# v projected in the attention's prologue instead of in the query stage (Mamba block, attention and experts on one core)

## The chip, the cores and the metric

The kernel runs on one core of a Trainium2 chip, in one launch. The metric is the device time of that core in microseconds (us), the median of several runs. A second number is used beside it: the span of one profiled execution, from its first to its last instruction. The engines are named as in the profile: PE is the matrix engine, PEld its weight loads, DVE the vector engine, ACT the scalar engine, POOL the GpSimd engine, and SP issues most of the DMA transfers.

## What is computed

The input x is 2 sequences of 2048 tokens, 256 wide. First x gets a Mamba block added (a selective scan over 512 channels and 16 states). Then follows the part that the change touches, and after it a layer of 8 experts, two of which each token uses:

```python
f = layernorm(x)                        # over the 256 features
a = rmsnorm(f) * ln1_w
q, k, v = a @ wq.T, a @ wk.T, a @ wv.T  # 16 heads of 16 columns
probs = softmax(q k^T / sqrt(16))       # per sequence and head, 2048 x 2048
h = f + (probs @ v) @ wo.T
out = x + h + moe(rmsnorm(h) * ln2_w)
```

## The kernel before, in words

The program has four stages, one after the other: `ssm_stage` (the Mamba block), `qkv_stage` (normalisation and the projections to q, k and v), `attention_stage` and `moe_stage`. Between `qkv_stage` and `attention_stage` all engines meet: the first stage's block ends when the last of its engines is done.

**`qkv_stage`.** It goes over 8 chunks of 512 tokens, c = 2i + b, where b is the sequence and i the chunk in it. The step of a chunk (`every_chunk`, `step`) has these parts, and each engine does its own in the order of its program:

- DVE makes the statistics and norms of the *next* chunk (`Normed.norms`, L1072 to L1096). It ends with `an`. On the way it waits twice for a square root from ACT (L1047, L1053).
- PE turns `an` (8 transposes, L1268) into `tr_ps`. ACT scales that with ln1_w into `aT` (L1219), which has two slots, one for each b. PE multiplies `aT` by wq and wk (L1279) into `qk_ps`.
- q and k leave as three bf16 parts whose sum is the float32 value. ACT casts the first part (L1227, once for q and once for k), DVE subtracts it (`rest`, L1306, twice), ACT casts the second part (L1253), and POOL makes the third (L1202, one instruction over 128 x 2048). SP stores each part to `parts` in memory (L1162).
- Last, PE multiplies `aT` by wv (L1287, 8 matmuls in the program, 16 in the records) into `v_ps`, and ACT copies that with 4 copies into `v_all` (L1236), where the attention takes it from.

At the end of the stage SP issues 16 loads of the first head's operands (`Lead.sync`, L1344). It may do so as soon as all chunks of b = 0 are stored. Then it issues the last chunk's 6 stores.

**`attention_stage`.** For each of 16 pairs of heads (both sequences), a head needs the maximum of its scores before their exponentials. So the maxima of a head are made while the head before it is computed, and those of the first head in a prologue. The maxima run through `ring`, a PSUM buffer of two slots s = 0, 1: for each of 16 key tiles t and each s, PE fills a slot with two matmuls (L1629), which use one half of the array's rows each, and DVE reduces it (L1752). PE may fill a slot again once DVE has reduced it. When the 32 reductions are done, DVE combines them (L1759), PE turns the row (L1636), ACT copies it (L1595), POOL splits it (L1552, L1554) and SP sends it to `qs` (L1513). The rest of the prologue is 8 fills for the second head. Then head 0 starts: scores (L1650) into `s_ps` (3 banks), exponentials on ACT (L1610), and values (L1662) from `vst`, which POOL copies out of `v_all` (`columns`, L1546) at the beginning of its prologue.

Of the kernel before, what the change touches and what calls it, by code (L numbers as in the profile page):

```python
# [1097 lines left out]
        last.then_inc(self.s_a, 1)  # L1098


def qkv_stage(nc, normed, f_dram, parts_dram, v_all, lead):
    B, L, _ = f_dram.shape
    NI = L // CH
    NC = B * NI
# [2 lines left out]
    with ExitStack() as ctx:  # L1107
# [6 lines left out]
        def sem(name):  # L1114
            return ctx.enter_context(nc.semaphore(name))

        wq, wk, wv = normed.w
        ln1, an, fo = normed.ln1, normed.an, normed.fo
        ident = normed.ident
        normed.second(ctx)  # L1120
        aT = sb("aT", [P, 2, KM, CH])
        part = sb("part", [P, 2, 3, 2 * KM, CH], BF16)
        rest = sb("rest", [P, 2, 2 * KM, CH])
        tr_ps = ps("tr_ps", [P, KM, CH])
        qk_ps = ps("qk_ps", [P, 2 * KM, CH])
        v_ps = ps("v_ps", [P, TT, DM])

        s_w, s_a, s_f, s_fst, s_tr = normed.s_w, normed.s_a, normed.s_f, normed.s_fst, normed.s_tr
        s_set = sem("q_set")
        s_aT = sem("q_aT")  # L1130
        s_qk = sem("q_qk")
        s_v = sem("q_v")
        s_p1 = sem("q_p1")
        s_r = sem("q_r")
        s_p2 = sem("q_p2")
        s_p3 = sem("q_p3")
        s_pst = lead.s_pst
        s_vout = sem("q_vout")

        block = ctx.enter_context(nc.Block())  # L1140

# [68 lines left out]
        @block.scalar  # L1210
        def _(act):
            act.wait_ge(s_w, 64)

            def take_aT(i, b):
                c = 2 * i + b
                wait(act, s_tr, c + 1)
                wait(act, s_v, c - 1)
                for k in range(KM):
                    nc.scalar.activation(aT[:, b, k, :], tr_ps[:, k, :], ACT.Identity,  # L1219
                                         scale=ln1[:, k:k + 1]).then_inc(s_aT, 1)  # L1220

            def first_part(i, b, m):
                c = 2 * i + b
                wait(act, s_qk, 2 * c + m + 1)
                wait(act, s_pst[b], 16 * 6 * i)
                at = slice(m * KM, (m + 1) * KM)
                nc.scalar.copy(part[:, b, 0, at], qk_ps[:, at, :]).then_inc(s_p1, 1)  # L1227

            def take_v(i, b):
                c = 2 * i + b  # L1230
                wait(act, s_v, c + 1)
                for t in range(TT):
                    dst = v_all[:, b * HP:(b + 1) * HP, bass.ds(i * TT + t, 1), :]
                    dst = dst.rearrange("p a o (h w) -> p (a o) h w", h=2)[:, :, :, 0:HD]
                    src = v_ps[:, t, :].rearrange("p (a h w) -> p a h w", h=2, w=HD)
                    last = nc.scalar.copy(dst, src)  # L1236
                last.then_inc(s_vout, 1)

            def front(i, b):
                take_aT(i, b)  # L1240

            def step(i, b, i2, b2):
                c = 2 * i + b
                if b2 is not None:
                    normed.first_root(act, i2, b2)
                first_part(i, b, 0)
                if b2 is not None:
                    normed.second_root(act, i2, b2)
                first_part(i, b, 1)
                if b2 is not None:  # L1250
                    take_aT(i2, b2)
                wait(act, s_r, 2 * (c + 1))
                nc.scalar.copy(part[:, b, 1], rest[:, b]).then_inc(s_p2, 1)  # L1253
                take_v(i, b)

            every_chunk(front, step, act)

        @block.tensor
        def _(pe):
            pe.wait_ge(s_w, 64)  # L1260

            def front(i, b):
                c = 2 * i + b
                wait(pe, s_a, c + 1)
                wait(pe, s_aT, 2 * c)
                for k in range(KM):
                    for t in range(TT):
                        last = nc.tensor.transpose(tr_ps[:, k, t * P:(t + 1) * P],  # L1268
                                                   an[b][:, t, k * P:(k + 1) * P], ident[:, :])
                last.then_inc(s_tr, 1)  # L1270

            def step(i, b, i2, b2):
                c = 2 * i + b
                wait(pe, s_aT, 2 * c + 2)
                for m, w in enumerate((wq, wk)):
                    wait(pe, s_r, 2 * c + m - 1)
                    for o in range(KM):
                        for k in range(KM):
                            last = nc.tensor.matmul(qk_ps[:, m * KM + o, :], w[:, k, o * P:(o + 1) * P],  # L1279
                                                    aT[:, b, k, :], start=(k == 0), stop=(k == KM - 1))  # L1280
                    last.then_inc(s_qk, 1)
                if b2 is not None:
                    front(i2, b2)
                wait(pe, s_vout, c)
                for t in range(TT):
                    for k in range(KM):
                        last = nc.tensor.matmul(v_ps[:, t, :], aT[:, b, k, t * P:(t + 1) * P], wv[:, k, :],  # L1287
                                                start=(k == 0), stop=(k == KM - 1))
                last.then_inc(s_v, 1)

            every_chunk(front, step, pe)

# [70 lines left out]
        self.lead(sp, 0, 0)  # L1363


def attention_stage(nc, parts_dram, v_all, att, B, L, lead):
    NP = B * HP
    QC = L // CH
    KT = L // P
    KK = 2 * KT  # L1370
    LEAD = 4
    assert QC == 4 and KT % 2 == 0 and NP % 2 == 0 and NP >= 6
    ROWS = 6 * HD + 2
    SC = float(HD) ** -0.5
    SR = 3
# [2 lines left out]
    with ExitStack() as ctx:  # L1378
# [36 lines left out]
        s_hi = sem("a_hi")  # L1415
        s_nmr = sem("a_nmr")
        s_on = sem("a_on")
        s_rec = sem("a_rec")

        LOADS = 16 * 2 * 2 * 6  # L1420
# [112 lines left out]
        def _(pool):  # L1533
# [29 lines left out]
                                        ALU.mult).then_inc(s_on, 1)  # L1563

            def prologue():
                columns(0, 0)
                rows_of_max(0, 1, None)

            def head(n, it, par, hh, has_prev, has_next, has_then):
                if hh == 1 and has_next:  # L1570
# [10 lines left out]
        @block.scalar  # L1581
        def _(act):
            def read_acc(n, hh):
                wait(act, s_pv, KK * n + KT * (hh + 1))
                nc.scalar.copy(osb[:, hh, :], acc[:, :]).then_inc(s_o, 1)

            def take_output(head, tile, nth):
                wait(act, s_S, taken(head, tile))
                wait(act, s_on, nth)
                nc.scalar.copy(oraw[:, :], s_ps[:, tile % SR, :]).then_inc(s_exp, 1)  # L1590

            def take_row(head, tile, nth):
                wait(act, s_S, nth if tile < 0 else taken(head, tile))
                wait(act, s_nmr, nth - 1)
                nc.scalar.copy(rowf[:, :], s_ps[0:KT, tile % SR, 0:P]).then_inc(s_exp, 1)  # L1595

            def prologue():
                take_row(0, -1, 1)

            def head(n, it, par, hh, has_prev, has_next, has_then):  # L1600
                u = 2 * n + hh
                for t in range(KT):
                    k = hh * KT + t
                    if t == 1 and has_prev:
                        read_acc(n if hh == 1 else n - 1, 1 - hh)
                    wait(act, s_pv, KK * n + k - PR + 1)
                    for j in range(QC):
                        tile = tile_of(t, j)
                        wait(act, s_S, taken(u, tile))
                        nc.scalar.activation(prob[:, k % PR, j, :], s_ps[:, tile % SR, :], ACT.Exp,  # L1610
                                             scale=SC).then_inc(s_exp, 1)
                    if t == T_OUT and has_prev:
                        take_output(u, I_OUT, u - 1)
                    if t == T_ROW and has_next:
                        take_row(u, I_ROW, u + 2)

            every_head(act, prologue, head)
            read_acc(NP - 1, 1)
            wait(act, s_S, TILES * 2 * NP)
            wait(act, s_on, 2 * NP - 1)  # L1620
            nc.scalar.copy(oraw[:, :], s_ps[:, 0, :]).then_inc(s_exp, 1)

        @block.tensor
        def _(pe):
# [28 lines left out]
            def values(n, par, k):  # L1653
# [9 lines left out]
                                            prob[:, k % PR, j, :], start=(t == 0), stop=(t == KT - 1))  # L1663
                last.then_inc(s_pv, 1)

            def prologue():
                ct = Count(0, start=True)
                pe.wait_ge(s_op4[0], LOADS4)
                for t in range(KT):
                    for s in range(2):  # L1670
                        maxima(ct, 0, t, s)
                pe.wait_ge(s_id, 2)
                rows_of_max(0, -1, 1)
                pe.wait_ge(s_op4[1], LOADS4)
# [816 lines left out]
def build(nc, a, out):  # L2491
# [8 lines left out]
    with ExitStack() as ctx:  # L2500
        s_x1st = ctx.enter_context(nc.semaphore("s_x1st"))
        with ExitStack() as ctx2:
            normed = Normed(nc, ctx2, x1, a["ln1_w"], a["wqT"], a["wkT"], a["wvT"], s_x1st)
            ssm_stage(nc, a["x"], a["W_inT"], a["vectors"], a["W_xT"],
                      a["W_outT"], x1, b_rows, normed, s_x1st)
            att = ctx2.enter_context(nc.sbuf_tensor("att", [P, L // P, B * HP, 2 * HD], F32))
            with ExitStack() as ctx3:
                v_all = ctx3.enter_context(nc.sbuf_tensor("v_all", [P, B * HP, L // P, VW], F32))
                lead = Lead(nc, ctx3, parts, L)
                qkv_stage(nc, normed, f, parts, v_all, lead)  # L2510
                attention_stage(nc, parts, v_all, att, B, L, lead)
            moe_stage(nc, f, att, a["woT"], a["ln2_w"], a["gateT"], a["w1T"], a["w2T"], a["w3T"], xg, out,
                      (normed.an[0], normed.fo[0]), normed.ident)

# [28 lines left out]
```

## Time and profile before

| | |
|---|---|
| runs | 3106.29, 3106.02, 3105.07 us, median 3106.02 us |
| profiled execution | 3123.07 us, its span 3121.2 us |
| mean granted PE clock | 0.962 of full speed |
| `qkv_stage` | from 1025.7 to 1131.2 us of the span |
| prologue of the attention | from 1131.2 to about 1177 us |
| busy PE, DVE, ACT, POOL over the span | 91%, 79%, 63%, 33% |

The profiled execution is one run with the profiler on; its time is 17 us above the median, so stretches are compared with stretches of the same trace. A timeline row gives the start, the time from the first start to the last end of merged instructions, engine, line, operation, what it writes and reads, their number, and in brackets how long the engine had been idle and what ended that. A row of stretches gives the stretch and its length, the busy time and number of instructions of PE, PEld, DVE, ACT and POOL, the granted clock, the DMA share and GB/s. The granted clock is a share of 2.4 GHz: 1.00 is 2.4 GHz and 0.50 is 1.2 GHz.

### The profile page before, as it was taken

To read this page: it belongs to the slowest core of one execution; us is meant where nothing else is said; L and a number is where in the kernel's file an instruction comes from. 1 tells how busy PE (TensorE), PEld (TensorE's weight loads), DVE (VectorE), ACT (ScalarE), POOL (GpSimd) and SP (SyncE) were. 2 spreads that over 40 slices of the span, in tenths; PEclk is the share of its full clock that TensorE was granted. 3 is DMA by queue.
4 is the path that set the end of the run, shared out by engine and by line. 5 is a ranking of instruction groups with operands and counts; after the bars stand their busy time and mean duration, and the time that the engine had idled before them with its cause. 6 is when DMAs were issued, how large, how long until landed. Compare 5 with 4: busy or idle time off the path is not lost. (4 is left out here: it accounts for less than half of the span.)

```text
span 3121.2 us, 48073 instructions
## 1 busy us (share of the span) xinstructions
PE 2835.9 (91%) x14250; PEld 1220.9 (39%) x14251; DVE 2461.2 (79%) x2883; ACT 1963.7 (63%) x3570; POOL 1033.5 (33%) x507
## 2 busy tenths in 40 slices
PE   8899889899866969999999999999999987499998
PEld 3344334444322522222222222222222226499997
DVE  5999999999999668888888888888888824444443
ACT  4676665665643426888787877878788873244443
POOL 4978878879763220000000000000000003422222
PEclk9999999999999979999999999999999997699999
DMA  2111111111111542111111011111111004533332
GB/s 68 38 53 58 38 51 58 41 51 51 41 44 40 187 124 41 42 42 34 40 42 36 25 35 42 42 42 39 35 42 42 11 25 157 184 50 49 48 48 37
DMA packets 125209, 169.40 MB, mean 54 GB/s; under 512 B 25552, under 2 KB 87760, under 8 KB 125008
## 3 DMA queue, kind: packets, MB, share of 16 engines
q1 hardware_dynamic: 110992, 148.19, 16.3%
q0 software_dynamic: 13440, 18.16, 3.4%
q8 instruction: 104, 1.70, 0.2%
q14 instruction: 97, 0.79, 0.1%
q10 hardware_dynamic: 576, 0.55, 0.1%
HBM read 125.80 MB, written 40.74 MB: 53 GB/s over the span
## 5 line engine op out<-in xcount | busy, mean ns | idle before, releaser
L1752 DVE TENSOR_REDUCE nmh<-ring 128x2 f32<-128x1024 f32 x1024 | 1196.0, 1219 | 178.2 <-PE ring L1629 177.9
L1610 ACT ACTIVATE prob<-s_ps 128x512 f32<-128x512 f32 x2048 | 1073.0, 603 | 281.9 <-PE s_ps L1650 281.9
L413 POOL TENSOR_TENSOR bx<-u,bb 128x2048 f32<-128x2048 f32 x127 | 574.3, 4528 | 171.7 <-DVE h L889 171.7
L1650 PE MATMUL s_ps<-qs,ks 98*128 98x512 bf16 x2048 | 612.8, 387 | 17.2 <-issue 11.6
L889 DVE TENSOR_TENSOR_SCAN h<-dA,state,bx 128x512 f32<-128x512 f32 x512 | 616.5, 1264 | 11.9 <-ACT dA L674 7.8
L674 ACT ACTIVATE dA<-dt,aneg 128x512 f32<-128x512 f32 x512 | 351.5, 690 | 316.5 <-DVE h L889 311.7
L1662 PE MATMUL acc<-prob,vst 128*32 128x512 f32 x4096 | 548.8, 608 | 0.2 <-ACT prob L1610 0.2
L743 PE MATMUL y_ps<-h,ident 128*128 128x512 f32 x1024 | 476.0, 609 | 1.1 <-DVE h L896 1.1
L1650 PEld LDWEIGHTS s_ps<-qs,ks 98*128 98x128 bf16 x2048 | 149.2, 97 | 579.5 <-ACT prob L1610 478.3
L1629 PE MATMUL ring<-k,q 64*128 64x512 bf16 x2048 | 347.9, 395 | 27.8 <-DVE nmh L1752 19.6
L896 DVE TENSOR_TENSOR h<-h,c_ps 128x2048 f32<-128x2048 f32 x128 | 289.7, 2263 | 3.5 <-PE c_ps L722 3.2
L743 PEld LDWEIGHTS y_ps<-h,ident 128*128 128x128 f32 x1024 | 200.3, 196 | 223.5 <-issue 216.3
L1552 POOL CAST nmr<-a_rowf 16x128 bf16<-16x128 f32 x32 | 9.0, 280 | 747.9 <-ACT a_rowf L1595 747.9
L1629 PEld LDWEIGHTS ring<-k,q 64*128 64x128 bf16 x2048 | 81.4, 93 | 377.5 <-issue 204.3
L1562 POOL TENSOR_TENSOR att<-oraw,rec 128x256 f32 (+1 forms) x32 | 19.8, 619 | 622.4 <-DVE rec L1766 622.4
L2088 POOL DMA_INDIRECT out_x<-fo,token x72 | 112.4, 1562 | 299.4 <-DVE fo L2453 296.5
L2470 DVE TENSOR_TENSOR an<-sl,up_ps 128x512 f32<-128x512 f32 x72 | 49.6, 689 | 186.5 <-ACT sl L2177 186.5
L2271 PE MATMUL t_ps<-m_xT,work 128*128 128x128 f32 x1152 | 142.2, 277 | 0.4 <-ACT work L2164 0.4
L2271 PE MATMUL up_ps<-m_xT,work 128*128 128x128 f32 x1152 | 141.0, 276 | 0.0
L2271 PEld LDWEIGHTS t_ps<-m_xT,work 128*128 128x128 f32 x1152 | 136.0, 194 | 0.9 <-issue 0.8
L2281 PE MATMUL t_ps<-w,an 128*128 x576 | 136.1, 379 | 0.0
L2271 PEld LDWEIGHTS up_ps<-m_xT,work 128*128 128x128 f32 x1152 | 135.1, 193 | 0.0
(253 smaller groups left out, 2496.9 us busy)
## 6 DMA issues: line engine op xcount, KB each, us to landing
bb<-b_rows SPq DMA_DIRECT2D x128, 256.0 KB, 3.1
q<-parts SPq DMA_DIRECT2D x256, 64.0 KB, 2.1
parts<-part SPq DMA_DIRECT2D x48, 256.0 KB, 2.5
qs<-parts SPq DMA_DIRECT2D x192, 64.0 KB, 2.9
ks<-parts SPq DMA_DIRECT2D x192, 64.0 KB, 2.9
xt<-slots_in SPq DMA_DIRECT2D x72, 133.0 KB
k<-parts SPq DMA_DIRECT2D x256, 32.0 KB, 2.0
fo<-in_x SPq DMA_DIRECT2D x8, 512.0 KB, 4.3
```

Of the source, the lines that this page charges most:

```text
L413: nc.gpsimd.tensor_tensor(bx[:, n % BR], u[:, b], bb[:, n % RB, None, :].to_broadcast([P, KI, CH]), ALU.mult).then_inc(s_bx, 1)
L674: nc.scalar.activation(dA[:, d % 2, :], dt[:, b, d, :], ACT.Exp, scale=aneg[:, d, n:n + 1]).then_inc(s_da, 1)
L743: last = nc.tensor.matmul(y_ps[:, d, :], ident[:, :], h[:, n % HR, d, :], start=False, stop=(n == NS - 1))
L889: nc.vector.tensor_tensor_scan(h[:, n % HR, d, :], dA[:, d % 2, :], bx[:, n % BR, d, :], state[:, b, n, d:d + 1], ALU.mult, ALU.add).then_ ...
L896: nc.vector.tensor_tensor(h[:, n % HR], h[:, n % HR], c_ps[:, None, :].to_broadcast([P, KI, CH]), ALU.mult).then_inc(s_hc, 1)
L1610: nc.scalar.activation(prob[:, k % PR, j, :], s_ps[:, tile % SR, :], ACT.Exp, scale=SC).then_inc(s_exp, 1)
L1629: ins = nc.tensor.matmul(ring[:, s, half, :], q4[r, slot, t * P:(t + 1) * P], k4[r, slot, s * CH:(s + 1) * CH], start=True, stop=True)
L1650: nc.tensor.matmul(s_ps[:, tile % SR, :], ks[:, par, hh, t * P:(t + 1) * P], qs[:, par, hh, j * CH:(j + 1) * CH], start=True, stop=True).t ...
L1662: last = nc.tensor.matmul(acc[32 * j:32 * j + 32, :], vst[:, par, t, v0:v0 + 32], prob[:, k % PR, j, :], start=(t == 0), stop=(t == KT - 1))
L1752: nc.vector.tensor_reduce(nmh[:, slot, t, 2 * s:2 * s + 2], ring[:, s, :, :], AX.X, ALU.max, negate=True).then_inc(s_free[s], 1)
L2271: last = nc.tensor.matmul(dst[:, q % 2, m * P:(m + 1) * P], wu[:, q % 2, w, k, m * P:(m + 1) * P], xT[:, q % 2, k, :], start=(k == 0), sto ...
L2281: last = nc.tensor.matmul(o_ps[:, q % 2, 0:DM], midT[:, q % 2, m, :], w2[:, bass.ds(e, 1), m, :].rearrange("p o n -> p (o n)"), start=(m = ...
```

## The change

`qkv_stage` no longer makes v. Its `v_ps` and the semaphores of v go away. `aT` is no longer a tile of two slots, but holds all 8 chunks: it lies in the memory of `att`, the attention's output, which is written only later. So ACT and PE address it in the loop by i. The attention's prologue makes v: after the two fills of key tile t, PE multiplies 256 tokens of `aT` by wv (`values_of`, 4 matmuls in the program, 8 in the records) into one of the three banks of `s_ps`, 16 groups in all, and ACT copies each with two copies into `v_all` (`take_v`). Before PE turns the row of maxima it now waits for all groups' copies, and POOL copies `columns` after the row of maxima, not before it.

```diff
@@ qkv_stage, scalar
                 wait(act, s_tr, c + 1)
-                wait(act, s_v, c - 1)
                 for k in range(KM):
-                    nc.scalar.activation(aT[:, b, k, :], tr_ps[:, k, :], ACT.Identity,
-                                         scale=ln1[:, k:k + 1]).then_inc(s_aT, 1)
+                    dst = aT[:, bass.ds(i, 1), b, k, :].rearrange("p o n -> p (o n)")
+                    nc.scalar.activation(dst, tr_ps[:, k, :], ACT.Identity, scale=ln1[:, k:k + 1]).then_inc(s_aT, 1)
...
                 nc.scalar.copy(part[:, b, 1], rest[:, b]).then_inc(s_p2, 1)
-                take_v(i, b)
@@ qkv_stage, tensor
                 if b2 is not None:
                     front(i2, b2)
-                wait(pe, s_vout, c)
-                for t in range(TT):
-                    for k in range(KM):
-                        last = nc.tensor.matmul(v_ps[:, t, :], aT[:, b, k, t * P:(t + 1) * P], wv[:, k, :],
-                                                start=(k == 0), stop=(k == KM - 1))
-                last.then_inc(s_v, 1)
@@ attention_stage, gpsimd
             def prologue():
+                rows_of_max(0, 1, None)
+                pool.wait_ge(s_vout, GROUPS)
                 columns(0, 0)
-                rows_of_max(0, 1, None)
@@ attention_stage, scalar
+            def take_v(group):
+                b, t0 = group // (KT // 2), 2 * (group % (KT // 2))
+                wait(act, s_v, group + 1)
+                for t in range(2):
+                    dst = v_all[:, b * HP:(b + 1) * HP, t0 + t, :].rearrange("p a (h w) -> p a h w", h=2)
+                    src = s_ps[:, group % SR, t * DM:(t + 1) * DM].rearrange("p (a h w) -> p a h w", h=2, w=HD)
+                    last = nc.scalar.copy(dst[:, :, :, 0:HD], src)
+                last.then_inc(s_vout, 1)
             def prologue():
+                for group in range(GROUPS):
+                    take_v(group)
                 take_row(0, -1, 1)
@@ attention_stage, tensor
+            def values_of(group):
+                b, t0 = group // (KT // 2), 2 * (group % (KT // 2))
+                wait(pe, s_vout, group - SR + 1)
+                for t in range(2):
+                    i, at = (t0 + t) // TT, (t0 + t) % TT * P
+                    for k in range(KM):
+                        last = nc.tensor.matmul(s_ps[:, group % SR, t * DM:(t + 1) * DM], aT[:, i, b, k, at:at + P],
+                                                normed.w[2][:, k, :], start=(k == 0), stop=(k == KM - 1))
+                last.then_inc(s_v, 1)
             def prologue():
                 ct = Count(0, start=True)
                 pe.wait_ge(s_op4[0], LOADS4)
                 for t in range(KT):
                     for s in range(2):
                         maxima(ct, 0, t, s)
+                    values_of(t)
+                pe.wait_ge(s_vout, GROUPS)
                 pe.wait_ge(s_id, 2)
                 rows_of_max(0, -1, 1)
```

The order of PE's program in the attention's prologue, before (128x512 is the shape of what a matmul writes; `nm` is the row of maxima):

```order
L1629 MATMUL ring<-k,q 128x512 x64
L1636 MATMUL s_ps<-a_ident,nm 16x128
L1629 MATMUL ring<-k,q 128x512 x16
L1650 MATMUL s_ps<-qs,ks 128x512 x2
```

and with the change, where the first pair of rows stands 16 times in all:

```order
L1623 MATMUL ring<-k,q 128x512 x4
L1666 MATMUL s_ps<-wv,att 128x256 x4
L1623 MATMUL ring<-k,q 128x512 x4
L1666 MATMUL s_ps<-wv,att 128x256 x4
...
L1630 MATMUL s_ps<-a_ident,nm 16x128
L1623 MATMUL ring<-k,q 128x512 x16
L1644 MATMUL s_ps<-qs,ks 128x512 x2
```

Between every four fills of `ring` now stand four matmuls of v.

ACT's program in the loop of `qkv_stage`, the step of an even chunk, before (ISA and REGISTER_ALU are register work):

```order
L1219 ACTIVATE aT<-tr_ps,ln 128x512 x2
L30 ISA
L1253 CAST part<-rest 128x2048
L1236 ISA
L1236 COPY v_all<-v_ps 128x8x2x16
L1236 ISA
L1236 COPY v_all<-v_ps 128x8x2x16
...
L1047 ACTIVATE q_sd<-q_mv,q_epsc 128x4
```

and with the change:

```order
L1215 ISA
L1215 ACTIVATE att<-tr_ps,ln 128x512
L1215 ISA
L1215 ACTIVATE att<-tr_ps,ln 128x512
L30 ISA
L1238 CAST part<-rest 128x2048
L30 ISA
L1047 ACTIVATE q_sd<-q_mv,q_epsc 128x4
```

The four copies of v are gone from between the cast and the square root, and a register instruction stands before each of the two writes of `aT`.

## Rows read from the trace of the kernel before

**Rows 1.** Busy time by stretch, a chunk of the query stage and the prologue.

```profile
1053.30:1065.10 11.80, 11.41 (x42) 6.83 (x41) 8.90 (x22) 6.76 (x11) 4.00 (x1) 1.00 0.66 214
...
1131.20:1168.30 37.10, 19.27 (x64) 3.28 (x64) 36.30 (x33) 0.00 (x0) 9.83 (x6) 0.50 0.29 78
```

**Rows 2.** Timeline of one chunk of the query stage, all engines.

```profile
1053.61 1.20 ACT L1236 COPY v_all<-v_ps 128x256 f32 x4 [0.44 <-PE v_ps L1287]
...
1059.43 1.14 DVE L1096 TENSOR_SCALAR an<-fo,q_rr 128x256 f32<-128x256 f32 x4 [0.20 <-DVE q_rr L1091]
1060.48 2.35 DVE L1306 TENSOR_TENSOR rest<-qk_ps,part 128x1024 f32<-128x1024 f32 x2
...
1060.70 1.09 PE L1268 MATMUL tr_ps<-ident,an 128*128 128x128 f32 x8 [0.39 <-DVE an L1096]
...
1061.63 3.62 PE L1287 MATMUL v_ps<-wv,aT 128*128 128x256 f32 x16
1061.83 1.26 ACT L1219 ACTIVATE aT<-tr_ps,ln 128x512 f32<-128x512 f32 x2 [0.47 <-PE tr_ps L1268]
...
1062.99 1.90 ACT L1253 CAST part<-rest 128x2048 bf16<-128x2048 f32 x1
...
1065.09 3.60 PE L1279 MATMUL qk_ps<-aT,wq 128*128 128x512 f32 x8
```

**Rows 3.** POOL's timeline: second, third and seventh of its eight subtractions.

```profile
1053.24 4.07 POOL L1202 TENSOR_TENSOR part<-rest,part 128x2048 bf16<-128x2048 f32 x1 [7.75 <-ACT part L1253]
1065.17 4.07 POOL L1202 TENSOR_TENSOR part<-rest,part 128x2048 bf16<-128x2048 f32 x1 [7.87 <-ACT part L1253]
...
1112.77 4.07 POOL L1202 TENSOR_TENSOR part<-rest,part 128x2048 bf16<-128x2048 f32 x1 [7.86 <-ACT part L1253]
```

**Rows 4.** DVE around POOL's second subtraction, and the same product without POOL beside it.

```profile
1008.13 0.16 DVE L1082 TENSOR_TENSOR q_ms<-q_mv,q_rs 128x4 f32<-128x4 f32 x1
...
1055.24 2.09 DVE L1082 TENSOR_TENSOR q_ms<-q_mv,q_rs 128x4 f32<-128x4 f32 x1
```

**Rows 5.** Timeline at the end of the query stage: SP and PE.

```profile
1119.78 0.35 SPq L1344 DMA_DIRECT2D q<-parts  x1
...
1127.13 3.56 SPq L1162 DMA_DIRECT2D parts<-part  x6
1131.24 1.04 PE L1629 MATMUL ring<-k,q 64*128 64x512 bf16 x4 [8.06 <-PEq L1107]
```

**Rows 6.** Timeline of the attention's prologue: PE, DVE and ACT.

```profile
1131.89 36.29 DVE L1752 TENSOR_REDUCE nmh<-ring 128x2 f32<-128x1024 f32 x32 [9.86 <-PE ring L1629]
1133.17 0.61 PE L1629 MATMUL ring<-k,q 64*128 64x512 bf16 x2 [0.89 <-DVE nmh L1752]
...
1165.97 0.61 PE L1629 MATMUL ring<-k,q 64*128 64x512 bf16 x2 [0.52 <-DVE nmh L1752]
1168.66 0.37 PE L1636 MATMUL s_ps<-a_ident,nm 128*16 128x128 f32 x1 [2.08 <-DVE nm L1759]
```

**Rows 7.** PE's timeline at full clock, in head 0 (starts tell the spacing).

```profile
1199.06 0.39 PE L1629 MATMUL ring<-k,q 64*128 64x512 bf16 x2
1199.38 0.82 PE L1650 MATMUL s_ps<-qs,ks 98*128 98x512 bf16 x3
1200.14 0.39 PE L1629 MATMUL ring<-k,q 64*128 64x512 bf16 x2
```

**Rows 8.** PE's timeline at the start of the query stage.

```profile
1025.88 1.07 PE L1268 MATMUL tr_ps<-ident,an 128*128 128x128 f32 x8 [1.81 <-PEq L67]
...
1028.36 5.31 PE L1279 MATMUL qk_ps<-aT,wq 128*128 128x512 f32 x8 [1.42 <-ACT aT L1219]
```

**Rows 9.** PE's first scores of head 0, and stretches around two rises of the clock.

```profile
1177.10 1.04 PE L1650 MATMUL s_ps<-qs,ks 98*128 98x512 bf16 x2
...
1028.40:1032.40 4.00, 4.00 (x6) 1.83 (x7) 1.78 (x8) 0.21 (x1) 0.00 (x0) 0.60 1.03 357
...
1184.40:1188.40 4.00, 3.62 (x21) 0.69 (x17) 2.38 (x3) 2.65 (x5) 0.00 (x0) 0.90 0.95 119
```

More of the change, by code:

```diff
@@ L1098, in norms, with qkv_stage @@
         last.then_inc(self.s_a, 1)
-def qkv_stage(nc, normed, f_dram, parts_dram, v_all, lead):
+def qkv_stage(nc, normed, f_dram, parts_dram, v_all, lead, aT):
     B, L, _ = f_dram.shape
@@ L1115, in sem @@
             return ctx.enter_context(nc.semaphore(name))
-        wq, wk, wv = normed.w
+        wq, wk = normed.w[0:2]
         ln1, an, fo = normed.ln1, normed.an, normed.fo
@@ L1120, in qkv_stage @@
         normed.second(ctx)
-        aT = sb("aT", [P, 2, KM, CH])
         part = sb("part", [P, 2, 3, 2 * KM, CH], BF16)
@@ L1125, in qkv_stage @@
         qk_ps = ps("qk_ps", [P, 2 * KM, CH])
-        v_ps = ps("v_ps", [P, TT, DM])
         s_w, s_a, s_f, s_fst, s_tr = normed.s_w, normed.s_a, normed.s_f, normed.s_fst, normed.s_tr
@@ L1131, in qkv_stage @@
         s_qk = sem("q_qk")
-        s_v = sem("q_v")
         s_p1 = sem("q_p1")
@@ L1137, in qkv_stage @@
         s_pst = lead.s_pst
-        s_vout = sem("q_vout")
         block = ctx.enter_context(nc.Block())
@@ L1227, in first_part @@
                 nc.scalar.copy(part[:, b, 0, at], qk_ps[:, at, :]).then_inc(s_p1, 1)
-            def take_v(i, b):
-                c = 2 * i + b
-                wait(act, s_v, c + 1)
-                for t in range(TT):
[L1233 to L1237, printed above, removed]
             def front(i, b):
@@ L1279, in step @@
                             last = nc.tensor.matmul(qk_ps[:, m * KM + o, :], w[:, k, o * P:(o + 1) * P],
-                                                    aT[:, b, k, :], start=(k == 0), stop=(k == KM - 1))
+                                                    aT[:, bass.ds(i, 1), b, k, :].rearrange("p o n -> p (o n)"),
+                                                    start=(k == 0), stop=(k == KM - 1))
                     last.then_inc(s_qk, 1)
@@ L1283, in step @@
                     front(i2, b2)
-                wait(pe, s_vout, c)
-                for t in range(TT):
-                    for k in range(KM):
-                        last = nc.tensor.matmul(v_ps[:, t, :], aT[:, b, k, t * P:(t + 1) * P], wv[:, k, :],
-                                                start=(k == 0), stop=(k == KM - 1))
-                last.then_inc(s_v, 1)
             every_chunk(front, step, pe)
@@ L1363, in sync, with attention_stage @@
         self.lead(sp, 0, 0)
-def attention_stage(nc, parts_dram, v_all, att, B, L, lead):
+def attention_stage(nc, normed, parts_dram, v_all, att, aT, B, L, lead):
     NP = B * HP
@@ L1371, in attention_stage @@
     LEAD = 4
-    assert QC == 4 and KT % 2 == 0 and NP % 2 == 0 and NP >= 6
+    assert B * KT // 2 == KT and QC == 4 and KT % 2 == 0 and NP % 2 == 0 and NP >= 6
     ROWS = 6 * HD + 2
@@ L1417, in attention_stage @@
         s_on = sem("a_on")
+        s_v = sem("a_v")
+        s_vout = sem("a_vout")
+        GROUPS = B * KT // 2
         s_rec = sem("a_rec")
@@ L2506, in build @@
             att = ctx2.enter_context(nc.sbuf_tensor("att", [P, L // P, B * HP, 2 * HD], F32))
+            aT = att[:, :, :, :].rearrange("p t a w -> p (t a w)")
+            aT = aT.rearrange("p (i b k n) -> p i b k n", b=B, k=KM, n=CH)
             with ExitStack() as ctx3:
@@ L2509, in build @@
                 lead = Lead(nc, ctx3, parts, L)
-                qkv_stage(nc, normed, f, parts, v_all, lead)
-                attention_stage(nc, parts, v_all, att, B, L, lead)
+                qkv_stage(nc, normed, f, parts, v_all, lead, aT)
+                attention_stage(nc, normed, parts, v_all, att, aT, B, L, lead)
             moe_stage(nc, f, att, a["woT"], a["ln2_w"], a["gateT"], a["w1T"], a["w2T"], a["w3T"], xg, out,
```

## The prediction

> **What bounds the kernel now.** I read the stretches first, to see which engine is full where v leaves and where it arrives. In a chunk of the query stage PE is busy 11.41 of 11.80 us, so it looks as if PE set the pace there; in the attention's prologue DVE is busy 36.3 of 37.1 us and PE only half of it, at a granted clock of 0.50 [rows 1]. The change looks right on both counts: it takes work from a full PE and gives it to a half idle one.
>
> The timeline of a chunk says otherwise. PE does not start its transposes when it is free, but when DVE's `an` is there: it idles 0.39 us before them [rows 2]. What `an` waits for is POOL. The small product `q_ms` (128 x 4) takes 0.16 us alone, but 2.09 us when it starts at 1055.24, and it ends at 1057.33; POOL's subtraction runs from 1053.24 to 1057.31 [rows 3, 4]. DVE stands still until POOL is done, whenever its product starts. So the chunk's period is a chain through DVE, ACT and POOL: `rest` ends at 1062.83; 0.16 later ACT's cast starts, 1.90; 0.28 later POOL starts, 4.07 [rows 2, 3]; from POOL's end (1057.31) to the end of `an` (1060.57) 3.26; from there to the end of `rest` 2.26 [rows 2, 4]. Sum 11.93 us. POOL's starts are (1112.77 - 1065.17)/4 = 11.90 us apart [rows 3]. v is in none of these terms.
>
> The stage's end is not PE's either. SP starts the first head's 16 loads at 1119.78, which need the parts that POOL made from 1112.77 on [rows 3, 5], issues the last stores until 1130.69, and then the attention starts, at 1131.24, with PE idle for 8.06 us [rows 5].
>
> In the prologue the reductions follow each other every 36.29/32 = 1.13 us, 2.26 per key tile [rows 6].
>
> **What leaves the query stage.** Per chunk PE loses 16 records of v. They start 3.46 us before the next matmuls, so 0.216 each [rows 2]. ACT loses four copies, 1.20 us [rows 2]. PE then waits for `aT`, which ends at 1063.09, and starts its next matmuls about 1.8 us earlier than 1065.09 [rows 2]. The cover that made v free is the DVE-POOL chain, and it stays: ACT's square root comes about 1.5 us earlier, so `q_ms` is issued earlier, but still after POOL has started, since the same cast precedes both [rows 2, 4]. The gain is **0 us** per chunk. The ends: 0, and PE's own loop if the chain did not bind (a rival below). The last chunk's v ended long before SP did [rows 5]: 0.
>
> **What the query stage gets.** ACT has a register instruction before each of its two writes of `aT`, and PE before two matmuls. PE's are covered by its new idle time. ACT's are not: `an`, transposes, `aT`, cast is a chain that ties with the one over `rest` (`aT` ends at 1063.09, the cast starts at 1062.99, `rest` ended at 1062.83 [rows 2]). No row prices them there. From below it is 0, since the second can go under the first write; from above 0.20 per chunk, DVE's idle time before `an` [rows 2]. I take 0.07, nearer to the lower end because ACT waits for the transposes anyway: 7 x 0.07 = **+0.5 us**, ends 0 and 1.4. The SP queue issues the same transfers in the same order.
>
> The clock of this stage can fall. Between the end of one chunk's q and k matmuls and the start of the next there will be about 4.7 us with only 1.1 us of transposes. At the stage's start PE had such a stretch, and the clock was at half for most of the 4 us that follow; the 8 matmuls then took 5.31 us, not 3.60 [rows 2, 8, 9]. That costs 1.7 us per chunk, against 1.8 us by which they start earlier: covered, and counted as 0.
>
> **What the prologue gets.** PE is to do 32 fills and 16 groups of 8 records of v. The clock decides. At 1.2 GHz a pair of fills streams for 0.43 us (its halves run side by side, 0.61 with the tail [rows 6]); at 2.4 GHz pairs end in 0.39 and the next group starts 0.32 later, 0.10 more than the 0.216 of a 512 column stream, and going back costs the same 0.10 ((1200.14 - 1199.38) - 3 x 0.22) [rows 7]. With v PE is nearly always streaming, so I expect 2.4 GHz after the start: the clock rose 3 to 4 us after dense matmuls began at 1028.36 [rows 8, 9].
>
> At full clock one key tile goes like this. From the first fill to its reduction 0.43 us (0.39 and 0.04), the second reduction starts 1.13 later, and its slot is refilled 1.28 after that (1133.17 - 1131.89 [rows 6]): 2.84 us from the first fill of a tile to the second fill of the next one. From there PE needs 0.32 for the fill and the change of kind, 8 x 0.216 = 1.73 for v and 0.10 to change back, 2.15 us, to the first fill of the tile after. Two tiles take 4.99 us, a tile **2.49 us** instead of 2.26. Neither engine is full: each waits for the other because the ring has only two slots. 16 x 0.23 = +3.7 us.
>
> The start is slower: at half clock a tile costs PE 2 x 0.43 + 2 x 1.73 + 0.2 = 4.5 us, so in the first 5 us it gets 1.1 tiles done, not 2.0; 0.9 x 2.49 = +2.2 us, ends 1.2 and 3.4 for a rise after 3 us, as there, or after 8, as in head 0, where scores began at 1177.10 and the clock rose about 1185.2 [rows 9]. At the end, the row of maxima turned 2.69 us after the last fill started (1168.66 - 1165.97 [rows 6]); now it waits for v, 2.05 us, the tail and semaphore, 0.2, and two copies on ACT, 0.6, with 0.1 behind them: 2.95, which is +0.3. The half clock's first tile had its first v wait covered by the first reductions: -0.6. Sum **+5.6 us**. ACT's 32 copies (0.6 per tile) are covered by the tile's 2.49. POOL's `columns` now stands behind the row of maxima; it is needed only by the first values of head 0, behind 8 more reductions of 1.13: 0. After that the order is the same, and head 0 starts at half clock in both; if it starts at the full one, up to 3 us come back.
>
> **The sum:** 0 + 0.5 + 5.6 = +6.1 us. Against the profiled execution 3123.1 + 6.1 = 3129.2; against the median of the runs, 17 us lower, 3106.0 + 6.1 = 3112.1, I say **3112.0 us**. A measurement of this kernel tells a change of about 0.2%, 6.2 us, from none, so the forecast lies at that edge.
>
> **The rivals.**
>
> *PE was the bound of the query stage.* The busy share speaks for it [rows 1]; the 0.39 us before the transposes and the 2.09 us product speak against it [rows 2, 4]. Then a chunk takes PE's loop: transposes to `aT` 1.13, `aT` 1.26, 16 matmuls at 0.43 6.9, handovers 0.3, sum 9.6, and 7 x 2.3 = 16.1 us come back: 3106.0 + 5.6 - 16.1 = 3095.5 us. Chance 0.07.
>
> *The prologue stays cheaper.* Changing kinds of matmul costs nothing (-1.5), the clock rises after 3 us (-1), and head 0 starts at full clock (-2): about +1.5, 3107.5 us. Chance 0.26.
>
> *The prologue is dearer.* Weight loads of v's float32 operand show behind a fill, where only bf16 changes have a row [rows 7]: 0.2 more per tile, half of which the coupling takes, and the clock rises late: +10, 3116 us. It decides once a tile takes over 2.55 us. Chance 0.20.
>
> *The clock of the query stage falls before the transposes too.* The row says that it fell in the stretch that held 8 transposes and idle time [rows 8, 9]. Where it covers the transposes of each chunk they take about 1 us longer on the chain: 7 us more, 3119 us. Chance 0.06. The Trainium skill speaks against the change here: its page "TensorE: Matmul & The Clock Gate", Part 4, says that a transpose on PE doesn't count as busy for the clock gate, so the whole gap would be idle for it. By that rule this rival comes out; in the row above the fall came after transposes, which agrees but doesn't prove it.
>
> *The clock never rises in the prologue,* as it did not rise there before [rows 1]. A tile costs 4.5 us: 16 x 2.24 = +36, 3142 us. Against it: v fills the gaps that kept PE half idle. Chance 0.03.
>
> **How the numbers follow.** The forecast's case (+4.5 to +8) has 0.38. Faster by over 0.2% is the first rival alone, 0.07. Slower is the dearer prologue, the two clock rivals and somewhat under half of the forecast's own case: 0.20 + 0.06 + 0.03 + 0.16 = 0.45. The rest, 0.48, is within 0.2%. The range runs from 3104 (the cheap prologue with all it can give back) to 3120 (the fallen clock), and leaves out PE's rival and the clock that never rises.
>
> **What would show it.** Right: POOL's subtractions still 11.9 us apart, `q_ms` still about 2 us and longer than before, PE idle about 3 us per chunk; the attention starting 105 to 107 us after the query stage; the 32 reductions spread over 41 to 44 us instead of 36.3; a granted clock of 1.00 in most of the prologue. Wrong: POOL's starts closer than 11.5 us, or reductions that still follow every 1.13 us.

## The result: 0.28% slower, by the prologue

Over 13 runs of each, the changed kernel took 3114.57 us and the kernel before 3105.78. The ratio is 1.0028, with a 95% interval of 1.0021 to 1.0036, so about 8.8 us more (6.5 to 11.2). The forecast was 3112.0. The runs of one kernel spread over 7 to 10 us, so the places are read from stretches inside one profiled execution. Over kernels with the same code there, they repeat within 0.3 us from the first fill on, and within 0.9 us in the query stage (106.44, 106.36 and 105.61 us in the changed kernel and in experiments 1 and 2):

| stretch | before | changed |
|---|---|---|
| query stage: PE's first transposes to its first fill of `ring` | 105.36 | 106.44 |
| prologue: first fill to the turned row of maxima | 37.42 | 44.02 |
| turned row to the first scores of head 0 | 8.44 | 8.11 |
| first scores to the first values | 6.09 | 6.10 |
| sum, us | 157.31 | 164.67 |

7.4 us of the loss stand here, 6.6 of them in the prologue. Of the 1.1 in the query stage 0.7 is one set of transposes that ran slowly once (experiment 7). The other 1.4 us are within the interval, and no stretch shows them: from its first to its last exponentials the attention took 1384 to 1390 us in the ten profiled executions, in no order by kernel. The totals of the profiled executions are not compared, since what follows the attention, which the change does not touch, took 559 us in that of the kernel before and 540 in that of the changed one, and the experiments show both lengths (540 in 1 to 4, 557 to 561 in 5 to 8).

The query stage after the change. First POOL's subtractions, the first four and the seventh (start, duration, engine, line, what, idle before and what ended it), to be laid beside [rows 3]:

```profile
1043.55 4.06 POOL L1198 TENSOR_TENSOR part<-rest,part 128x2048 bf16<-128x2048 f32 x1 [14.74 <-ACT part L1238]
1056.11 4.06 POOL L1198 TENSOR_TENSOR part<-rest,part 128x2048 bf16<-128x2048 f32 x1 [8.49 <-ACT part L1238]
1068.13 4.07 POOL L1198 TENSOR_TENSOR part<-rest,part 128x2048 bf16<-128x2048 f32 x1 [7.96 <-ACT part L1238]
1080.02 4.06 POOL L1198 TENSOR_TENSOR part<-rest,part 128x2048 bf16<-128x2048 f32 x1 [7.82 <-ACT part L1238]
...
1115.92 4.07 POOL L1198 TENSOR_TENSOR part<-rest,part 128x2048 bf16<-128x2048 f32 x1 [7.96 <-ACT part L1238]
```

They are 12.56, 12.02 and 11.89 us apart, and (1115.92 - 1056.11)/5 = 11.96 on average from the second on. PE lost 3.46 us of work per chunk and the chunk did not get shorter. The small product that waits for POOL shows why. This is the answer for the tile `q_ms` in the changed kernel (number, shortest, median and longest in ns, first and last start):

```profile
L1082 DVE TENSOR_TENSOR q_ms<-q_mv,q_rs x6: 3716/3771/3936, 1043.9 to 1104.2; 128x4 f32<-128x4 f32 x6
```

Beside POOL's subtraction it starts about 1.6 us sooner than before, and it takes 1.6 us longer (3.7 against 2.09 in [rows 4]): it still ends when POOL ends.

The prologue after the change, its start, a steady piece and its end, PE and DVE:

```profile
1134.36 1.03 PE L1623 MATMUL ring<-k,q 64*128 64x512 bf16 x4 [13.32 <-PEq L1107]
...
1135.33 3.78 PE L1666 MATMUL s_ps<-wv,att 128*128 128x256 f32 x8
...
1139.04 1.04 PE L1623 MATMUL ring<-k,q 64*128 64x512 bf16 x4
...
1141.93 0.61 PE L1623 MATMUL ring<-k,q 64*128 64x512 bf16 x4
...
1142.36 4.82 DVE L1758 TENSOR_REDUCE nmh<-ring 128x2 f32<-128x1024 f32 x4 [0.32 <-PE ring L1623]
1142.47 1.99 PE L1666 MATMUL s_ps<-wv,att 128*128 128x256 f32 x8
...
1144.39 0.77 PE L1623 MATMUL ring<-k,q 64*128 64x512 bf16 x4
...
1145.09 1.99 PE L1666 MATMUL s_ps<-wv,att 128*128 128x256 f32 x8
...
1147.02 0.61 PE L1623 MATMUL ring<-k,q 64*128 64x512 bf16 x4
...
1147.45 4.82 DVE L1758 TENSOR_REDUCE nmh<-ring 128x2 f32<-128x1024 f32 x4 [0.28 <-PE ring L1623]
...
1174.94 0.78 PE L1623 MATMUL ring<-k,q 64*128 64x512 bf16 x4
...
1178.38 0.28 PE L1630 MATMUL s_ps<-a_ident,nm 128*16 128x128 f32 x1 [0.74 <-ACT v_all L1586]
```

and the stretches up to and from the rise of the clock (PE, PEld, DVE, ACT, POOL busy, granted clock, DMA share, GB/s):

```profile
1134.30:1140.10 5.80, 5.74 (x17) 2.91 (x17) 2.77 (x3) 0.65 (x2) 5.66 (x4) 0.51 0.66 175
1140.10:1178.40 38.30, 37.56 (x177) 24.18 (x177) 35.14 (x31) 9.71 (x30) 3.59 (x2) 1.00 0.21 50
```

The first two tiles, at 1.2 GHz for most of the time, take 1141.93 - 1134.36 = 7.57 us. Two tiles of the steady part took 4.52 before: +3.0. (The first two tiles before took less, 4.19 us, because both slots are free at the start. Against them it is +3.4, and the end gives 0.4 back.) The 13 tiles from there to the last take 1174.94 - 1141.93 = 33.0, so 2.54 each against 2.26: +3.6. In the steady piece DVE's reductions come in fours, with a gap of 0.27 us before the next four. PE waits less. It goes from fill to fill in 1144.39 - 1141.93 = 2.46 us in one tile and 1147.02 - 1144.39 = 2.63 us in the next, where the four fills take 0.77 us instead of 0.61 because a slot is not free yet. So PE's own work alone would take about 2.46 us per tile, 0.20 more than DVE's 2.26, and the waits for each other add only the last 0.08. The turned row waited for ACT's last copy, as the last row says, but by little: it came 1178.38 - 1174.94 = 3.44 us after the last tile's first fill, against 3.82 before, and DVE had finished the row of maxima only 0.3 us earlier, at 1178.07.

### The profile page after: what moved, and what is told of

Its sections match the earlier page's. It is cut to its first block and busy times, and to the rows that moved or that the text cites. A ratio compares the mean times of both kernels' runs of the same rounds, so it can differ in the third digit from the quotient of the medians.

```text
span 3115.0 us, 48067 instructions
## 1 busy us (share of the span) xinstructions
PE 2846.5 (91%) x14250; PEld 1223.7 (39%) x14251; DVE 2471.8 (79%) x2883; ACT 1964.3 (63%) x3570; POOL 1033.5 (33%) x507
## 5 line engine op out<-in xcount | busy, mean ns | idle before, releaser
L743 PE MATMUL y_ps<-h,ident 128*128 128x512 f32 x1024 | 483.9, 617 | 1.1 <-DVE h L896 1.1
L1623 PE MATMUL ring<-k,q 64*128 64x512 bf16 x2048 | 340.0, 388 | 17.4 <-PEq L1107 13.3
```

What stands on the lines that cost most here:

```text
L743: last = nc.tensor.matmul(y_ps[:, d, :], ident[:, :], h[:, n % HR, d, :], start=False, stop=(n == NS - 1))
L1623: ins = nc.tensor.matmul(ring[:, s, half, :], q4[r, slot, t * P:(t + 1) * P], k4[r, slot, s * CH:(s + 1) * CH], start=True, stop=True)
```

## The experiments

Experiments 1 to 4 were timed beside the kernel before at 3105.95 us, 5 to 8 beside it at 3126.93 us; a ratio is always to the runs of the kernel before that were made beside it. Times of stretches are those of the table above.

### 1. No v at all

```diff
-                    values_of(t)
-                pe.wait_ge(s_vout, GROUPS)
...
-                for group in range(GROUPS):
-                    take_v(group)
...
-                nc.gpsimd.memset(v_all[:, :, :, col:col + 1], 1.0).then_inc(s_set, 1)
+                nc.gpsimd.memset(v_all[:, hh * HP:(hh + 1) * HP, :, :], 1.0).then_inc(s_set, 1)
```

> The changed kernel without v: no matmuls and no copies of v anywhere, v_all is set to ones. It tells what the query stage alone gives. Theory 1 (the pace of the query stage is the chain DVE, ACT, POOL): POOL's subtractions 11.9 to 12.1 us apart as in the changed kernel, the prologue back at 37.4 us from the first fill to the turned row, so the kernel before + 1 us (+0 to +2), and 7 to 8 us faster than the changed kernel. Rival (PE was the bound of the query stage): 9.6 us per chunk, 15 us faster than before.

Measured: 1.0004 (0.9995 to 1.0013). The query stage took 106.36 us, the prologue 37.42, the whole stretch 158.30, which is 1.0 above the kernel before. A kernel that makes no v at all is not faster than one that makes it in the query stage. So v was free where it stood, and the rival (15 us faster) is out.

### 2. Half of v in the prologue

```diff
-                    for k in range(KM):
-                        last = nc.tensor.matmul(s_ps[:, group % SR, t * DM:(t + 1) * DM], aT[:, i, b, k, at:at + P],
-                                                normed.w[2][:, k, :], start=(k == 0), stop=(k == KM - 1))
+                    last = nc.tensor.matmul(s_ps[:, group % SR, t * DM:(t + 1) * DM], aT[:, i, b, 0, at:at + P],
+                                            normed.w[2][:, 0, :], start=True, stop=True)
```

> The changed kernel with half of v's matmuls: only the first 128 of the 256 features are summed; groups, copies, waits and changes of kind stay. Theory 1 (two slots of the ring couple PE and DVE: two tiles cost the 2.84 us of the reductions plus what PE does after the refill): 2.84 + 0.3 + 0.86 + 0.3 = 4.3 us is under DVE's own 4.52, so the reductions follow every 1.13 us once the clock is up, prologue 37.4 + 1 to 3 us, the kernel 4 to 5 us faster than the changed one. Rival (each group has a fixed cost by its waits, its weight loads or ACT's reads of PSUM beside DVE's): tiles stay at about 2.5 us, no gain over the changed kernel beyond 1 us.

Measured: 1.0002 (0.9993 to 1.0011), prologue 38.60 us, 5.4 less than with all of v. Once the clock is up, the reductions run as before, here ten in 11.40 us:

```profile
1138.51 0.61 PE L1623 MATMUL ring<-k,q 64*128 64x512 bf16 x4
1138.94 11.40 DVE L1757 TENSOR_REDUCE nmh<-ring 128x2 f32<-128x1024 f32 x10 [0.38 <-PE ring L1623]
```

The groups, their waits, their changes of kind and ACT's copies are all still there and cost nothing here. What costs is PE's time between two fills once it is longer than the reductions leave it. The 1.2 us that stay are about the start at half clock. This experiment does not tell the coupling by two slots from PE's own time: the shorter groups bring PE's own time to about 1.6 us per tile as well, also under DVE's 2.26. The rows of the result tell them apart (2.46 and 2.54 us), and a ring with a third slot was not tried.

### 3. and 4. POOL's subtraction behind DVE's norms

In the kernel before (3) and in the changed one (4):

```diff
             def third_part(i, b, norms_after=True):
...
+                if norms_after:
+                    wait_apart(pool, s_a, c + 3, s_w)
                 nc.gpsimd.tensor_tensor(part[:, b, 2], rest[:, b], part[:, b, 1], ALU.subtract).then_inc(s_p3, 1)
```

The last two subtractions have no norms to wait for. They stand behind the loop without the new wait.

> The kernel before with one more wait: POOL's subtraction of chunk c waits until DVE has made an of chunk c + 2 (so that DVE's norms are never beside POOL's read). All is computed. Theory 1 (POOL's subtraction holds DVE's norms up): q_ms takes 0.16 us again, the chain gets shorter than PE's work, and PE's 11.4 us per chunk bind: 0.3 to 0.5 us per chunk, 2 to 3.5 us faster than before. Rival (DVE's long q_ms is something else, POOL is not what it waits for): POOL's work is only later, the chunk gets longer by up to 4 us, 0 to 28 us slower than before.

> The changed kernel with the same wait of POOL. Theory 1: with the chain shortened, PE has room (no v) and the chunk falls to 9.7 to 10.5 us: 10 to 15 us faster than the changed kernel, 1 to 6 us faster than the kernel before. Together with the run before this one it tells that v's matmuls cost the query stage something only where the chain does not bind. Rival (PE's own loop or the clock binds near 11.9): under 3 us faster than the changed kernel.

Measured (3): 0.9997 (0.9988 to 1.0006), which alone says nothing. The stretches do: the query stage took 102.53 us, 2.8 less, and `q_ms` takes 0.16 us:

```profile
L1082 DVE TENSOR_TENSOR q_ms<-q_mv,q_rs x6: 161/162/164, 1044.1 to 1100.2; 128x4 f32<-128x4 f32 x6
```

Measured (4): 0.9993 (0.9984 to 1.0003), against 1.0028 for the change without the wait; the query stage took 98.74 us, 7.7 less than in the changed kernel. POOL made to wait makes the stage shorter, in both kernels, so POOL's work beside the norms was what held them. And v's matmuls show their price now: with the chain shortened, the stage takes 3.8 us longer with v (102.53) than without (98.74).

The gain is under the 10 us that I had expected, and the trace of (4) says where it went. Third to fifth of POOL's subtractions, and PE's and DVE's rows around them:

```profile
1067.78 4.08 POOL L1200 TENSOR_TENSOR part<-rest,part 128x2048 bf16<-128x2048 f32 x1 [6.59 <-DVE an L1096]
1080.27 4.08 POOL L1200 TENSOR_TENSOR part<-rest,part 128x2048 bf16<-128x2048 f32 x1 [8.40 <-DVE an L1096]
1090.45 4.09 POOL L1200 TENSOR_TENSOR part<-rest,part 128x2048 bf16<-128x2048 f32 x1 [6.10 <-DVE an L1096]
```

```profile
1060.91 1.40 DVE L1072 BATCH_NORM_STATS2 q_stats<-xa 128x6 f32<-128x256 f32 x4 [1.52 <-DMA xa<-out_x]
...
1064.87 1.01 ACT L1226 CAST part<-qk_ps 128x1024 bf16<-128x1024 f32 x1 [1.74 <-DMA parts<-part]
...
1070.49 6.77 PE L1267 MATMUL qk_ps<-att,wq 128*128 x8 [1.63 <-ACT att L1219]
```

A good chunk takes 10.18 us, but one took 12.49: its q matmuls ran 6.77 us instead of 3.70, since the granted clock had fallen to 0.51 from 1069.9 to 1076.8. In the changed kernel the fallen clock was hidden by the chain; here nothing hides it. Besides, DVE now waits for the load of x and ACT for the stores of the part before. I read this as SP's queue being late next, since it sends the third part later (not tried apart).

### 5. and 6. Seven groups of v at the end of the query stage

In the changed kernel (5) and together with the waiting POOL (6). PE idled 13.3 us before the first fill; seven of the 16 groups are put there, nine stay between the maxima.

```diff
+TAIL = 7
...
             every_chunk(front, step, pe)
+            for group in range(TAIL):
+                wait(pe, s_vout, group - 1)
...
+                        last = nc.tensor.matmul(v_ps[:, group % 2, t * DM:(t + 1) * DM], aT[:, i, b, k, at:at + P],
+                                                wv[:, k, :], start=(k == 0), stop=(k == KM - 1))
+                last.then_inc(s_v, 1)
```

> The changed kernel, but 7 of v's 16 groups are made at the end of the query stage, after PE's last q and k matmuls, where PE idled 13.3 us until SP had issued its transfers; 9 groups stay between the maxima. All is computed. Theory 1: the 12 us of the 7 groups are hidden by SP; of the prologue's 6.6 us over the kernel before, 9 tiles x 0.28 = 2.5 us stay and the cold start goes (the clock may still fall before the first fill, then up to 2 us stay), prologue 40 to 42 us: 3 to 5 us faster than the changed kernel. Rival (the prologue is dearer by something that v brings once, as the copies or the last wait): 1 us faster at most.

> Both together: 7 groups of v at the end of the query stage, and POOL's subtraction behind the norms. All is computed. Theory 1: the query stage takes 98 to 99 us as with the waiting POOL alone (106.4 in the changed kernel), the prologue 40 to 42: 11 to 13 us faster than the changed kernel, 4 to 6 us faster than the kernel before. Rival (the two gains share one cover, the end of the stage): the query stage takes over 101 us.

Measured (5): 1.0012 (1.0003 to 1.0021), query stage 106.95 us, prologue 39.67. The prologue's loss fell from 6.6 to 2.25 us, for nine tiles at 0.28 and no slow start. PE's rows at the end of the query stage:

```profile
1119.59 3.62 PE L1291 MATMUL v_ps<-wv,att 128*128 128x256 f32 x16
...
1124.59 8.90 PE L1291 MATMUL v_ps<-wv,att 128*128 128x256 f32 x40 [1.38 <-ACT v_all L1253]
...
1134.48 0.61 PE L1646 MATMUL ring<-k,q 64*128 64x512 bf16 x4 [0.99 <-PEq L1110]
...
1137.64 1.99 PE L1689 MATMUL s_ps<-wv,att 128*128 128x256 f32 x8
```

The four fills at 1134.48 take 0.61 us, the length at full clock, not 1.03. So seven groups are worth 7 x 0.28 = 2.0 us and the warm start about the other 2.4. The groups cost something in return. SP issued its last store by 1132.5, but the copies of the last group on ACT end at 1134.2, and the attention starts behind them. From POOL's last subtraction to the first fill it is 10.36 us, against 8.95 in the changed kernel: 1.4 us lost at the hand-over.

Measured (6): 0.9986 (0.9977 to 0.9995), query stage 97.23, prologue 39.66, the whole stretch 151.41 us: 5.9 less than the kernel before and 13.3 less than the changed one. It computes everything and is faster than both kernels; over the kernel before the ratio gives about 4.4 us (1.6 to 7.2).

### 7. The chunk loop written out

```diff
-            with eng.Fori(1, NI) as i:
+            for i in range(1, NI):
                 step(i - 1, 1, i, 0)
                 step(i, 0, i, 1)
```

> The changed kernel with the chunk loop of PE, DVE and ACT in the query stage written out, so that no register instruction stands before the writes and reads of aT. Theory 1: the 0.1 us per odd chunk by which POOL's subtractions are farther apart than in the kernel before (12.02 against 11.93) are ACT's register instruction behind the wait; they go: 0.3 to 0.6 us off the query stage, in the total not to be told from noise. Rival (they come from PE's clock or from the idle PE's later start): spacing stays 12.0 and 11.9.

Measured: 1.0017 (1.0008 to 1.0026), not told apart from the changed kernel's 1.0028 (1.0021 to 1.0036). POOL's spacings were 12.07, 12.01, 11.95, 12.06, 11.89: their sum did not fall. The rival was right about the spacing, theory 1 about the link. From the start of the transposes to ACT's first write of `aT` it is 1.22 us in every later chunk of the changed kernel, 1.13 and 1.20 in turn before, and 1.11 here where the clock is up; the register instruction is gone. But in three of six chunks the transposes now run slowly:

```profile
1062.17 1.04 PE L1252 MATMUL tr_ps<-ident,an 128*128 128x128 f32 x8
...
1074.08 1.56 PE L1252 MATMUL tr_ps<-ident,an 128*128 128x128 f32 x8 [2.35 <-DVE an L1096]
...
1086.13 1.05 PE L1252 MATMUL tr_ps<-ident,an 128*128 128x128 f32 x8
```

1.56 us against 1.05: half a microsecond, and it is on the chain. The changed kernel itself had this once, 1.81 us in its second chunk, which is most of the 12.56 us there; at the same place experiment 1 had 12.51, experiments 2 and 5 11.83 and 11.82.

### 8. Eight groups at the end, with the waiting POOL

```diff
-TAIL = 7
+TAIL = 8
```

> As the run with both, with 8 groups (the whole first sequence) at the end of the query stage and 8 in the prologue. Theory 1: PE's idle time there, 15.1 us with the waiting POOL, still covers 13.8 us, and the prologue loses one more tile's 0.28 us: 0 to 0.5 us faster than with 7, not to be told in the total. Rival (the copies of the last groups end after SP and hold the stage's end): 1 us slower than with 7.

Measured: 0.9985 (0.9976 to 0.9994). The prologue took 39.46 us, 0.2 less than with seven groups, the query stage 98.41, 1.2 more, the whole 152.39. The chunks are not the reason: from the first transposes to POOL's last subtraction it is 86.27 us with eight groups and 86.44 with seven. From there to the first fill it is 12.14 against 10.79, so all of the loss stands there. With eight groups the last two copies on ACT run from 1123.38 on for 0.65 us, 1.6 us beyond SP's last store (1122.38), and the first fill comes at 1124.33. With seven they ended at 1119.39, before SP did (1119.53). So the rival was right: the eighth group no longer fits into the idle time. In the total of the runs seven and eight are not told apart.

```profile
1118.84 3.54 SPq L1164 DMA_DIRECT2D parts<-part  x6
1123.38 0.65 ACT L1257 COPY v_all<-v_ps 128x256 f32<-128x256 f32 x2 [1.08 <-PE v_ps L1295]
1124.33 0.61 PE L1650 MATMUL ring<-k,q 64*128 64x512 bf16 x4 [0.99 <-PEq L1110]
```

## Why the prediction held, step by step

- **"The gain is 0 us per chunk."** Right, and experiment 1 shows it directly. The chain over `rest`, ACT's cast, POOL and the norms sets the chunk; the product is issued earlier and only waits longer. Experiment 3 shows the cause: without POOL beside it, the same product takes 0.16 us and the stage shrinks.
- **The register instructions, +0.5.** They are 0.1 us on one link in every other chunk, so about 0.3 in all. The size was small enough not to matter, and in experiment 7, which removes it, slower transposes took the gain away.
- **"Covered, and counted as 0", the clock in the query stage.** Half right. The granted clock did fall there: 0.74 over the chunk from 1051.9, 1.00 over the next. In the q and k matmuls it is hidden, as said: 5.39 us instead of 3.70 in every second chunk, at the price given (1.7), with POOL's subtractions no farther apart for it than the register instruction explains. In the transposes it is not; in the profiled run it cost 0.7 us once. The rival that had it in each chunk (+7) didn't come. By the Trainium skill's rule (the page "TensorE: Matmul & The Clock Gate", Part 4) transposes don't count as busy, from which the prediction took that this rival would come. Here PE's clock fell in about every second chunk, and no run tells the transposes' share in that from the idle time around them.

```profile
1051.90:1063.90 12.00, 10.18 (x24) 4.50 (x23) 10.00 (x23) 5.04 (x7) 4.06 (x1) 0.74 0.64 205
1063.90:1075.90 12.00, 8.17 (x26) 3.77 (x25) 10.70 (x23) 5.98 (x8) 4.07 (x1) 1.00 0.70 219
...
1066.31 3.70 PE L1263 MATMUL qk_ps<-att,wq 128*128 x8 [1.65 <-ACT att L1215]
1078.34 5.39 PE L1263 MATMUL qk_ps<-att,wq 128*128 x8 [1.63 <-ACT att L1215]
```

- **"A tile 2.49 us instead of 2.26", +3.7.** The path was right, the size 0.05 short: 2.54. From the start of a group to the next fill it is 1147.02 - 1145.09 = 1.93 us, so 0.20 above 8 x 0.216, not 0.10. The 0.10 that was left out is at the start of the group: its second record starts 0.32 us after the first. It stands once in the path over two tiles, so a tile gets half of it. Experiment 2 fits the sum: with 0.86 us less between two fills the tile falls to DVE's own time, and not below. But the words "neither engine is full: each waits for the other" explain only 0.08 of the 0.28 us. PE's own 2.46 us per tile is 0.20 above DVE's 2.26 without any wait for a slot; by the prediction's own terms it was 0.22 + 0.32 + 1.73 + 0.10 = 2.37, already above 2.26. Of the 2.46 us 0.30 are the changes of kind (last section), so fewer and longer groups might have stayed under 2.26; this was not tried.

```profile
1142.47 0.48 PE L1666 MATMUL s_ps<-wv,att 128*128 128x256 f32 x1
...
1142.79 0.59 PE L1666 MATMUL s_ps<-wv,att 128*128 128x256 f32 x2
```

- **The slow start, +2.2, less 0.6.** The forecast was 1.6 beyond the tiles' own loss. Measured: +3.4 over the first two tiles, 2.8 beyond the tiles' own loss (about 2.4 by experiment 5, which also has the end as before). The clock rose at 1140.1, 5.7 us after the first fill, within the 3 to 8 us given. The -0.6 for a first wait that the reductions cover was wrong: the first tile at half clock took 4.68 us. With 1.2 us this is the term that was mis-sized most.
- **The wait at the end, +0.3.** The wait was there, but the last tile's start to the turned row is 3.44 us against 3.82 before: 0.4 us less, 0.7 less with that tile's own loss taken off, so 1.0 below the forecast. That this nearly offsets the slow start is luck: in the sum of the prologue (+6.6 against +5.6) mostly the tile's 16 x 0.05 us is left to see.
- **Head 0 "starts at half clock in both".** Right: its first scores take 1.04 us at 1186.49 as they did at 1177.10, and the 3 us did not come back.
- **The sum.** +6.1 was forecast, +7.4 stands in the stretches and +8.8 in the medians. I called slower by over 0.2% slightly less likely than no change (0.45 against 0.48); with the tile and the start at the size that they had, it would have been the likelier.

## What to carry to other kernels

A busy share near 1 doesn't make an engine the bound: look at what ends its last idle time, and at instructions that take many times their usual duration, since they show a wait that is counted as work. Work under such a chain is free where it stands. Moving it beside another engine's work costs as soon as the time that it adds between two refills no longer fits into that engine's pace. Here PE's own 2.46 us per tile had passed DVE's 2.26, and the ring of two slots added 0.08. If the chain can be cut, do that first; then the freed engine is worth something, and long waits on a queue (here PE's 13 us before the attention) are the place for the work, as long as it ends before the queue does.

## What the runs showed of the hardware

A vector product over 4 elements per partition with two inputs from SBUF stood still for as long as POOL's subtraction ran: 0.16 us alone, 2.1 or 3.8 us beside it, always ending with it. A reciprocal (one input) beside POOL's subtraction from 1053.24 on [rows 3] took its usual 0.18 us:

```profile
1055.02 0.18 DVE L1079 RECIPROCAL q_rs<-q_sd 128x4 f32<-128x4 f32 x1 [2.19 <-ACT q_sd L1047]
```

In the changed kernel a subtraction of `rest`, with one of its inputs in PSUM, took its usual 1.23 us at 1118.76, beside POOL's from 1115.92 on.

Between pairs of matmuls that use half of the array's rows each and full float32 ones, at full clock, a change cost 0.2 us into the float32 ones and 0.1 us back. From the second pair to the group it is 1142.47 - 1142.16 = 0.31 us instead of 0.22, from the group's first record to its second 0.32 instead of 0.216, and from its last to the next fill 1144.39 - 1144.08 = 0.31.

And taking work away from PE can cost: with gaps in it the granted clock fell to 1.2 GHz in about every second chunk of the changed kernel. Its eight q matmuls then took 5.39 us instead of 3.70, which the chain hid. In experiment 4 they once took 6.77 us, and nothing covered them.
